# Block 1's edge pass: GpSimd takes the remainders of the odd quads

## The reference

```python
h = jnp.maximum(_layernorm(x, axis=-1), 0.0)
msg = relu(concatenate([x[row], x[col]], axis=-1) @ W.T + b)   # one row of 64 per edge
agg = segment_sum(msg, row, num_segments=x.shape[0])
out = relu(concatenate([x, agg], axis=-1) @ W.T + b)
```

## Time and profile before

| | |
|---|---|
| three executions, median | 16102.5 us |
| the profiled execution: span from first to last instruction | 16121.7 us |
| VectorE's remainders in this pass: first to last start | 5087.0 to 5824.8 us |
| one group of four quads, where the clock is full | 7.06 us |
| GpSimd busy over the whole span | 70% |

### The profile page before, as it was taken

One profiled execution on the slowest core, in us unless ns is written; L12 is line 12 of the kernel. 1 busy time (PEld: TensorE's weight loads), 2 busy tenths in 40 slices (PEclk: granted clock), 3 DMA queues, 4 the chain that ended last, 5 costly groups with the idle time before them and its releaser, 6 DMA issues. The chain is left out here.

```text
span 16121.7 us, 259900 instructions
## 1 busy us (share of the span) xinstructions
PE 8240.4 (51%) x75452; PEld 7447.2 (46%) x75452; DVE 6705.2 (42%) x24185; ACT 5671.5 (35%) x13374; POOL 11290.4 (70%) x11862
## 2 busy tenths in 40 slices
PE   6555551566554753444432443441444444788886
PEld 4545541555554643333322333331444443777775
DVE  5555553777775863333344333334222224111112
ACT  2555551777774531222211222220211111333331
POOL 4777767677775457777767777767777773777773
PEclk9777765877887975666665666665555555999996
DMA  4444441322223743444432444432322221444441
GB/s 154 161 161 161 161 137 56 98 93 93 90 92 137 257 135 103 147 146 145 145 106 86 146 145 145 145 125 58 85 84 84 84 82 53 142 145 145 145 146 51
DMA packets 887810, 1965.20 MB, mean 122 GB/s; under 512 B 384390, under 2 KB 463440, under 8 KB 846481
## 3 DMA queue, kind: packets, MB, share of 16 engines
q1 hardware_dynamic: 418593, 797.27, 14.4%
q0 software_dynamic: 361120, 582.27, 14.3%
q10 hardware_dynamic: 107776, 582.40, 9.4%
HBM read 1095.90 MB, written 894.54 MB: 123 GB/s over the span
## 5 line engine op out<-in xcount | busy, mean ns | idle before, releaser
L112 POOL DMA_INDIRECT eg_got<-gat_table,eg_rows x4992 | 4726.6, 947 | 1541.5 <-issue 1494.8
L112 POOL DMA_INDIRECT e_got<-table,e_rows x3328 | 3159.5, 949 | 1029.9 <-issue 1004.0
L1321 PE MATMUL eg_ps_sum<-eg_got,eg_equal 128*128 128x136 f32 (+1 forms) x9984 | 2076.7, 383 | 274.1 <-DVE eg_got L1409 252.4
L1328 ACT ACTIVATE eg_outs<-eg_ps_sum 128x544 f32<-128x544 f32 (+1 forms) x1248 | 676.1, 542 | 4282.9 <-PE eg_ps_sum L1321 4270.6
L1321 PEld LDWEIGHTS eg_ps_sum<-eg_got,eg_equal 128*128 128x128 f32 x9984 | 1971.5, 292 | 337.5 <-ACT eg_outs L1328 182.8
L117 POOL DMA_INDIRECT sorted_rows<-sort_rows,sort_dest x1664 | 1621.2, 974 | 533.3 <-issue 499.2
L1353 PE MATMUL eg_small<-ident,eg_score 128*128 128x128 f32 (+1 forms) x312 | 138.6, 444 | 3176.0 <-DVE eg_score L1392 3176.0
L1353 PEld LDWEIGHTS eg_small<-ident,eg_score 128*128 128x128 f32 (+1 forms) x312 | 47.1, 151 | 3203.4 <-DVE eg_score L1392 3203.4
L1390 DVE TENSOR_TENSOR eg_diff<-eg_small,eg_got 128x128 f32<-128x128 f32 (+1 forms) x312 | 79.1, 254 | 2736.3 <-DMA eg_got<-gat_table,eg_rows 2736.3
L1587 DVE TENSOR_SCALAR e_got<-e_ps_second 128x512 f32<-128x512 f32 x416 | 287.8, 692 | 1828.8 <-PE e_ps_second L1570 1807.4
L567 PE MATMUL e_ps_sum<-e_got,e_equal 128*128 128x64 f32 x3328 | 630.2, 353 | 677.9 <-DMA e_got<-table,e_rows 677.9
(11 more groups left out here) (524 smaller groups left out, 21304.8 us busy)
## 6 DMA issues: line engine op xcount, KB each, us to landing
gat_out<-eg_outs ACTq DMA_DIRECT2D x208, 1152.0 KB
eg_equal_b<-equal_d SPq DMA_DIRECT2D x312, 512.0 KB
out<-e_outs ACTq DMA_DIRECT2D x208, 512.0 KB
out<-e_outs ACTq DMA_DIRECT2D x104, 1024.0 KB
values<-e_zeros_b SPq DMA_DIRECT2D x104, 768.0 KB
values_q<-e_zeros_b SPq DMA_DIRECT2D x104, 768.0 KB
sort_value<-values_q SPq DMA_DIRECT2D x104, 768.0 KB
e_value<-values SPq DMA_DIRECT2D x104, 768.0 KB
```

What stands on the lines that cost most here:

```text
L112: return e.indirect_dma_start(out, None, table, bass.IndirectOffsetOnAxis(ap=index, axis=0), **kw)
L1321: last_i = e.matmul(ps_sum[q % 2][:, i, 0:FG], equal[q % 4][:, i, :], got[k][:, t, :], start=True, stop=True)
L1328: e.activation(outs[k % 2][:, tiles, 0:FG], ps_sum[q % 2][:, :, 0:FG], ACT.Copy).then_inc(copied.sem, 1)
```

## The change

VectorE makes the remainders of even quads only, as before. For odd quads ScalarE makes one more activation, the relu in f32, into the buffer `rest`; then it makes the first part as before; then GpSimd subtracts the first part from it in place. `less` becomes `less_even` and `less_odd`; the relu counts on a new semaphore `relued`. ScalarE takes over the wait that the odd remainder's buffer be free (`cut_3` of the quad four earlier). SyncE's load of new rows waits for the even remainders and for the first parts, where it waited for all remainders.

```diff
@@ sync
-                    e.wait_ge(less.sem, less.at(it, (k + 1) * QUADS - U))
+                    e.wait_ge(less_even.sem, less_even.at(it, ((k + 1) * QUADS - U) // 2))
+                    e.wait_ge(cut_1.sem, cut_1.at(it, (k + 1) * QUADS - U))
@@ vector
-            def rests(it, q):
-                k, tiles, _ = place(q)
-                e.wait_ge(cut_1.sem, cut_1.at(it, q + 1))
-                e.wait_ge(cut_3.sem, cut_3.at(it, q + 1 - n4))
-                e.scalar_tensor_tensor(rest[q % 4][:, :, :], rows[k][:, tiles, 1:], 0.0, cut[q % CUTS][:, 0], ALU.max, ALU.subtract).then_inc(less.sem, 1)
+            def even_rests(it, q):
+                if q % 2 == 0:
+                    k, tiles, _ = place(q)
+                    e.wait_ge(cut_1.sem, cut_1.at(it, q + 1))
+                    e.wait_ge(cut_3.sem, cut_3.at(it, q + 1 - n4))
+                    e.scalar_tensor_tensor(rest[q % 4][:, :, :], rows[k][:, tiles, 1:], 0.0, cut[q % CUTS][:, 0],
+                                           ALU.max, ALU.subtract).then_inc(less_even.sem, 1)
...
-            stepped(e, (3, rests), (5, add), (7, compare))
+            stepped(e, (3, even_rests), (5, add), (7, compare))
@@ scalar, first_part
                 e.wait_ge(added.sem, added.at(it, q + 1))
                 e.wait_ge(summed.sem, summed.at(it, q + 1 - CUTS))
+                if q % 2:
+                    e.wait_ge(cut_3.sem, cut_3.at(it, q + 1 - n4))
+                    e.activation(rest[q % 4][:, :, :], rows[k][:, tiles, 1:], ACT.Relu).then_inc(relued.sem, 1)
                 e.activation(cut[q % CUTS][:, 0], rows[k][:, tiles, 1:], ACT.Relu).then_inc(cut_1.sem, 1)
@@ scalar, second_part
-                e.wait_ge(less.sem, less.at(it, q + 1))
+                less = less_odd if q % 2 else less_even
+                e.wait_ge(less.sem, less.at(it, q // 2 + 1))
@@ gpsimd
+            def odd_rests(it, q):
+                if q % 2:
+                    e.wait_ge(relued.sem, relued.at(it, q // 2 + 1))
+                    e.wait_ge(cut_1.sem, cut_1.at(it, q + 1))
+                    e.tensor_tensor(rest[q % 4][:, :, :], rest[q % 4][:, :, :], cut[q % CUTS][:, 0], ALU.subtract).then_inc(less_odd.sem, 1)
...
-            stepped(e, (1, third_part))
+            stepped(e, (3, odd_rests), (1, third_part))
```

More of the change, by code:

```diff
@@ L1075, in carried_pass @@
         added = Tally(ph, "added", U, ahead=2)
-        cut_1 = Tally(ph, "cut_1", U)
-        less = Tally(ph, "less", U, ahead=U)
+        cut_1 = Tally(ph, "cut_1", U, ahead=U)
+        relued = Tally(ph, "relued", U // 2)
+        less_even = Tally(ph, "less_even", U // 2, ahead=U // 2)
+        less_odd = Tally(ph, "less_odd", U // 2)
         cut_2 = Tally(ph, "cut_2", U)
@@ L1168, in vector @@
             e.sem_inc(added.sem, added.ahead)
-            e.sem_inc(less.sem, less.ahead)
-            stepped(e, (3, rests), (5, add), (7, compare))
+            e.sem_inc(less_even.sem, less_even.ahead)
+            stepped(e, (3, even_rests), (5, add), (7, compare))
             keys.links(e)
@@ L1198, in scalar @@
             e.sem_inc(copied.sem, copied.ahead)
+            e.sem_inc(cut_1.sem, cut_1.ahead)
             stepped(e, (2, second_part), (4, first_part), (0, copy_sums))
```

## The result

The changed kernel takes 16050.65 us (median of 7, 16046.59 to 16062.85); the kernel before took 16101.29 us beside it (7 executions, 16093.5 to 16102.71). The ratio is 0.997, 95% interval [0.996, 0.9981]. That is 50.6 us faster, where 57 were forecast.

A forecast was written before the change was run, and what follows sets the result against it. No engine is full; a closed chain through VectorE, TensorE and ScalarE sets 7.06 us a group. 104 x 0.58 = 60 us, less 3 for the clock, gives 57: 16102.5 - 57 = 16045.5 us, range 16030 to 16090.

The forecast's parts named there:

- The closed chain: From remainder n (n a group's first quad) to remainder n+4, through VectorE, TensorE and ScalarE: sets the 7.06 us a group.
- The signs given: In the trace: remainders n to n+4 6.4 to 6.6 us apart, VectorE's wait near 1.7, no relu wait for GpSimd.
- Remainder n+1 and the relu of n+3: Second quad's remainder leaves VectorE, last quad's relu joins ScalarE: copy n-1 starts 0.58 us earlier, 60 us over 104 groups.
- the DMA stretch: ScalarE from copy n-1 through three DMA issues to remainder n+4: 2.75 us with 0.05 ahead of the copy, unchanged.
- The relu's pace: ScalarE's added f32 relu, start to start: 0.30 us taken, with bounds 0.28 and 0.58.
- rival A: ScalarE's relu is dear, its waits and register steps not hidden: gain 28 us, 16074 us; chance 0.13.
- ScalarE ends last: Ahead of copy n-1: ScalarE ready at 5304.06, TensorE would allow 5303.97, so the gain is 0.58 us a group.
- The ceiling of 67 us: Largest gain, with all of 0.67 us a group, unless TensorE is faster than 1.10 us a quad.
- rival B: GpSimd becomes the new wait, odd remainder and waits over 1.17 us: at 1.5, 16079 us; chance 0.08.
- slack of 0.5 us: GpSimd's third part n-1, queued behind odd remainder n+1, would still end 0.5 us before sums n-1 need it.
- Falls of the clock, 3 us: About 12 short falls to 1.2 GHz over the pass, TensorE losing some 0.25 us more in each: 3 us.
- Rival C: Slower by the clock: busier TensorE makes half-clock falls frequent; at 40% of groups 35 us slower, 16138 us; chance 0.06.

The follow-up runs named there:

- experiment 1: Against the kernel before, only the remainder of each group's second quad (n+1) goes to GpSimd, with one f32 relu a group: 16040.79 us, ratio 0.9961.
- 2: Against the kernel before, only the remainder of each group's last quad (n+3) goes to GpSimd, with one f32 relu a group: 16099.21 us, ratio 0.9999.
- experiment 3: The changed kernel with ScalarE's f32 relu of quad n+3 made twice, the second into a spare tile: 16068.21 us, ratio 0.9978 to the kernel before.
- 4: The changed kernel with an additional f32 relu on ScalarE in quad n+1, into a spare tile: 16031.29 us, ratio 0.9955 to the kernel before.
- experiment 5: The kernel before with each group's three output DMAs issued by SyncE and no longer by ScalarE: 15932.7 us, ratio 0.9897.
- experiment 9: The kernel before with SyncE's load of new rows issued after ScalarE's DMA issues: an undisturbed group 7.06 us, as before; 20309.9 us on a slower chip.
- experiment 11: The changed kernel with 64 one-column copies on ScalarE ahead of the loop: 6.69 us median across the turn's end; 20101.1 us on a slower chip.

## Why the prediction came out right

**The closed chain: right.** 7.06 us was read as VectorE 3.39, TensorE 0.92 and ScalarE 2.75. Experiments 1 and 2 show that only the remainder at its place counts, 3 and 4 that only ScalarE's work between two certain copies does, and 5 that its DMA issues do. The signs given came too, but for the period, which at 6.34 us is a little under the 6.4 to 6.6 announced: VectorE waits for the first part once a group, 1.60 us in an undisturbed one, ScalarE's relu never waits for GpSimd, and GpSimd's remainders take 0.68 us on average.

**Remainder n+1 and the relu of n+3, 0.58 us a group: right.** With 1.80 us put for the DMA stretch the chain as predicted gives 7.06 - 0.58 - 0.14 = 6.34, which is what was measured. The relu's pace was 0.30 to 0.31 in the trace and 0.30 in experiment 3; the upper bound of 0.58 (rival A) is out. That ScalarE ends last, and not TensorE, was right by a hair: TensorE needs 1.17 us for a quad and not the 1.10 that I read off, so the copy of n-1 could have started at most 0.03 us earlier. (The 0.16 us that I took off the 1.26 is idle time of the weight loads' row; TensorE as a whole lost only 0.09 us there.) By my own numbers TensorE and ScalarE were not level either at the relu's lower bound: ScalarE would have ended at 5304.04, TensorE at 5303.97. The ceiling of 67 us rested on the 1.10 and was too high by some 7 us, as experiment 1 shows.

**GpSimd: right for this kernel, its slack overrated.** A remainder takes 0.67 us, as taken from the third part, which is 1.6 times VectorE's 0.41; that is less than the factor of two with which I said it agreed. The wait for it that rival B fears is not in the changed kernel's trace. But of the slack of 0.5 us only 0.27 held when it was drawn on, since third part n-1 then met the remainder that I had placed outside the chain.

**The DMA stretch: a term that I had at "unchanged".** It fell by 0.14 us in an undisturbed group, and that is most of the 12 us by which the 72 of the table above are over the 60 forecast. Issuing SyncE's load later did not shorten it (experiment 9). The edge rows' issues took 0.62 us in the kernels in which GpSimd makes both remainders n+1 and n+3, in some groups with n+3 alone, and in the first group of a turn in the kernel before; elsewhere they took 0.72 to 0.77. Why is open.

**The turn's end and the clock: the term that was mis-sized.** "Falls of the clock, 3 us" was 23 us. The turn's end, which the sum did not have at all, went from 0.33 to 0.65 us or a little more on ScalarE (9 us in all). The falls to the 1.2 GHz level came 16 times instead of 12, all at the turn's end, and cost 0.88 us each there (14 us). TensorE's wait at the turn's end, about 2.1 us, comes ahead of each of them, but it doesn't explain them by itself: 9 of the 25 turns have that wait and no fall, experiment 3 has waits of about 1.95 us in 24 turns and 4 falls there, and the kernel before has its 12 falls with no wait of TensorE over 1.71 us up to where the pass runs dry. Rival C had the clock down to 0.9 or less from TensorE's being busier. Being busier does not do it: with TensorE busy 278 us of 300 (experiment 5) the clock is 1.00, and in the changed kernel the fall shown above comes right behind a wait of 2.11 us.

The Trainium skill (Runtime: NRT & Kernel Launch, Instruction fetch mechanics) says that a taken branch whose target is not in the current window of two pages stalls for a fetch; it gives a page 256 instructions. The trace counts 143 instructions of ScalarE in a turn before and 166 after, so the loop fits that window and the rule does not account for what is seen: a cost at the loop's branch of 0.33 us at best and about twice that in some kernels. The 64 copies of experiment 11 did not bring the long one back, so it does not repeat in steps of 16, 32 or 64 instructions. Nothing here shows a fetch itself.

So the sum put the gain of the groups 12 us too low and the losses 20 us too low. The two errors offset each other for the most part: the pass gave 48 us where 57 were forecast. That the whole came within 6 us of the forecast is partly luck.

## What to carry to other kernels

When no engine is full, follow one instruction from a group to the same instruction of the next group, and list what lies between: only work on that closed chain is worth moving, and the same edit two quads further on is worth nothing. Look in the chain for DMA issues on a compute engine's queue; moving them to SyncE, which had time for them, was worth 168 us here, three times the change under study. And before a difference of 0.1% is put down to an edit in a loop, shift the loop by a few instructions and look again.

The fastest kernel of the study is the changed one with its stores on SyncE, 15928.4 us, level with the kernel before with the same stores, 15932.7; with its code unshifted and its stores on ScalarE the change gives 50.6 us, four copies ahead of the loop 19 more, and moving n and n+1 instead of the odd quads 22 more.

## What the runs showed of the hardware that was not expected

- Three DMA issues on ScalarE hold it for 1.5 us between two activations (1.43 to 1.58 us of idle time), 0.33 us more across the loop's branch, and about twice that in some kernels, by the place of their code as far as the runs tell.
- Four one-column copies ahead of a loop made the kernel 19 us faster (16031.27 against 16050.65 us).
- A subtraction on GpSimd and a remainder on VectorE lock each other out in part: a third part that starts 0.02 to 0.04 us behind a remainder takes 0.89 to 0.90 us instead of 0.67.
- The DMA engines moved 345 GB/s at a share of 0.97, with three kinds of transfers of 0.5 to 0.8 MB.
